# Three-product projections and logits in a gated-scan and expert kernel on one core

## The reference

```python
x  = hidden_states                      # (2, 1024, 256)
xn = layernorm(x)                       # no weights
# attention part
k  = xn @ W_z.T + b_z
log_z, log_coeffs = -softplus(-k), -softplus(k)
log_values = concat([g_log(h0), log_z + g_log(xn @ W_h.T + b_h)], axis=1)
a_star = pad(cumsum(log_coeffs, axis=-1))
log_h  = a_star + cumlogsumexp(log_values - a_star, axis=1)
log_h  = (log_h - log_h.mean()) / std(log_h)        # over everything
attn   = layernorm(exp(log_h)[:, 1:] + xn) * ln_w + ln_b
# expert part
w, e   = top_k(softmax(xn @ w_gate.T), 2); w = w / w.sum()
ffn    = sum over the 2 experts of  w * ((silu(xn @ w1.T) * (xn @ w3.T)) @ w2.T)
out    = x + attn + ffn
```

## Time and profile before

| | |
|---|---|
| median of three runs | 357.22 us |
| the profiled execution | 357.79 us, span 356.1 us |
| granted TensorE clock, mean | 0.969 |
| TensorE busy | 325.8 us, 91% of the span |
| VectorE busy | 260.8 us, 73% |
| ScalarE busy | 219.9 us, 62% |
| GpSimd busy | 206.4 us, 58% |
| chain of waits | TensorE 54%, VectorE 23%, ScalarE 8% |

### The profile page before, as it was taken

How to read it: one execution, slowest core, us unless ns; L and a number is a source line. 1 busy time by engine, 2 the same in 40 slices (tenths; PEclk the granted TensorE clock), 3 DMA queues, 4 the chain that set the end, 5 groups by cost and what they waited for, 6 DMA issues and landing times.

```text
span 356.1 us, 6682 instructions
## 1 busy us (share of the span) xinstructions
PE 325.8 (91%) x1964; PEld 273.9 (77%) x1964; DVE 260.8 (73%) x466; ACT 219.9 (62%) x328; POOL 206.4 (58%) x137
## 2 busy tenths in 40 slices
PE   8998999799999999999898999999999999979830
PEld 8883464588878898997787899889898988969730
DVE  5488787989996899889899842584589668763300
ACT  2547997455879974999854269934853485323400
POOL 4500023159968674989899728563885475945331
PEclk9999969989999999999999999999999999999985
DMA  7924912005444542354354434542463534354621
GB/s 263 426 120 137 293 52 59 15 11 150 122 82 115 142 101 32 80 129 129 44 144 109 102 38 115 142 101 33 84 181 89 75 45 76 47 76 49 98 38 15
DMA packets 19086, 37.00 MB, mean 104 GB/s; under 512 B 2272, under 2 KB 13536, under 8 KB 19008
## 3 DMA queue, kind: packets, MB, share of 16 engines
q0 software_dynamic: 9168, 11.97, 21.5%
q1 hardware_dynamic: 8496, 22.56, 20.4%
q10 hardware_dynamic: 1376, 1.85, 1.4%
HBM read 27.45 MB, written 11.03 MB: 108 GB/s over the span
## 4 chain that ended last, share of the span: by engine, by line
PE 54%; DVE 23%; ACT 8%; issue 8%; DMA 2%; ACTq 1%; POOL 1%; POOLq 0%; DVEq 0%
PE PS L1296 23%; PE PS L1314 11%; PE PS L1190 6%; PE PS L1326 5%; DVE wrow L1067 3%; DVE tmp L961 3%; PE PS L1176 2%; DMA out<-work,sidx 2%; DVE hT L956 2%; DVE U L985 2%; DVE A L998 1%; PE PS L1220 1%; DVE xrow L1054 1%; DVE xrow L1059 1%; PE PS L1265 1%
## 5 line engine op out<-in xcount | busy, mean ns | idle before, releaser
L1296 PE MATMUL PS<-wbuf,xT 128*128 128x512 f32 (+1 forms) x648 | 149.6, 384 | 4.9 <-issue 3.7
L1296 PEld LDWEIGHTS PS<-wbuf,xT 128*128 128x128 f32 x648 | 118.3, 190 | 29.4 <-issue 9.3
L424 POOL TENSOR_TENSOR wbuf<-raw,wbuf x28 | 81.4, 2924 | 23.1 <-ACT wbuf L604 21.4
L406 POOL DMA_INDIRECT out<-work,sidx x35 | 62.7, 1792 | 53.2 <-ACT work L621 20.1
L1314 PE MATMUL PS<-wbuf,hT 128*128 128x256 f32 x648 | 86.8, 288 | 0.0
L1314 PEld LDWEIGHTS PS<-wbuf,hT 128*128 128x128 f32 x648 | 79.3, 189 | 1.9 <-issue 1.9
L390 POOL DMA_INDIRECT work<-xn_dram,gidx x39 | 50.4, 1292 | 51.8 <-DVE gidx L892 36.1
L595 ACT ACTIVATE tmp<-PS 128x512 f32<-128x512 f32 x72 | 32.0, 460 | 41.6 <-PE PS L1296 41.3
L961 DVE TENSOR_TENSOR tmp<-tmp,PS 128x512 f32<-128x512 f32 x72 | 35.0, 516 | 29.4 <-ACT tmp L595 28.6
L956 DVE TENSOR_TENSOR hT<-PS,hT 128x768 fp32r<-128x768 f32 x36 | 34.2, 949 | 29.3 <-ACT hT L590 24.2
L621 ACT ACTIVATE work<-PS,wrow 128x256 f32<-128x256 f32 x35 | 16.4, 470 | 38.0 <-PE PS L1314 38.0
(11 more groups left out here) (185 smaller groups left out, 350.7 us busy)
## 6 DMA issues: line engine op xcount, KB each, us to landing
raw<-w_main SPq DMA_DIRECT2D x24, 544.0 KB
raw<-w_main SPq DMA_DIRECT2D x8, 416.0 KB
xn_dram<-xrow SPq DMA_DIRECT2D x4, 516.0 KB, 7.2
out<-xrow POOLq DMA_DIRECT2D x4, 512.0 KB, 6.1
xrow<-x SPq DMA_DIRECT2D x4, 256.0 KB, 4.8
xrow<-x ACTq DMA_DIRECT2D x4, 256.0 KB, 5.4
small_sb<-small ACTq DMA_DIRECT2D x1, 768.0 KB, 7.9
work<-xn_dram,gidx POOLq DMA_INDIRECT x39
```

The source lines that it names most:

```text
L406: pool.indirect_dma_start(out, bass.IndirectOffsetOnAxis(sidx[:, j:j + 1], 0), ysb[:, j % DEEP, :], None, compute_op=ALU.add).then_inc(s_s ...
L424: pool.tensor_tensor(lo, raw[:, ds(part, WP)], hi.bitcast(fp32), ALU.subtract).then_inc(s_w, 1)
L1296: ins = pe.matmul(PS[:, at:at + cols], xT[:, slot, xpart, q * P:(q + 1) * P], wbuf[:, w, wpart, q * 2 * F + at:q * 2 * F + at + cols], sta ...
```

## The change

Nothing of the result changes in form; three things change in how the first stage computes it.

- **Products.** The transposed input is kept as a high and a low part (`xnT_parts`, in the half of `wbuf` that the second expert fills later). ScalarE's evacuation writes the high part, VectorE subtracts it from PSUM for the low part (`xnT_low`). The projection weights and the gate weights are split too (`wzh_hi`, `wzh_lo`, `wg_parts`). A projection of 512 columns by 128 inputs becomes three "r" products (high with high, low weight with high x, high weight with low x). For the logits one product takes high x with 16 columns (both parts of the gate weights), another low x with 8; an addition joins the two sums.
- **Groups.** The first normalisation goes in eight groups of two tiles; ScalarE and GpSimd normalise one each. Fillers stand in rounds 0 to 3, the chunk-0 projections, all of them, in rounds 4 to 7.
- **Order on VectorE.** The low parts stand between the statistics and between the first expert's pieces; its third and fourth low piece go behind the tables. The one-hot tile moves from `hT` to `wbuf`.

Low parts of the input stand between the pieces, two low pieces have left this place, and the routing has one operation more. The diff, cut to its core:

```diff
-        xnT = xnT_M[:, :].rearrange("p (q n) -> p q n", q=Q)
...
+        xnT_parts = wflat[:, 2 * WALL:2 * WALL + 4 * NTOK].rearrange("p (c n q t) -> p c n q t", c=NCH, n=2, q=Q)
...
-        onehot_tile = hT[:, :, :].rearrange("p a n -> p (a n)")[:, 0:2 * NT * NCOL]
+        onehot_tile = wflat[:, 2 * WALL:2 * WALL + 2 * NT * NCOL]
+        hflat_r = hT[:, :, :].rearrange("p a n -> p (a n)")
+        wzh_hi = hflat_r[:, 0:4 * D].rearrange("p (q m d) -> p q m d", q=Q, m=2)
+        wzh_lo = [v.rearrange("p (m d) -> p m d", m=2) for v in (hflat_r[:, 4 * D:6 * D], wflat[:, 2 * WALL + 4 * NTOK:2 * WALL + 4 * NTOK + 2 * D])]
...
+        wg_parts = sb("wg_parts", [P, Q, 2, E], f32r)
...
-        logit_ps = PS[:, 7 * 512:7 * 512 + NT * E]
+        logit_ps = PS[:, 7 * 512:7 * 512 + 2 * NT * E].rearrange("p (t n e) -> p t n e", n=2, e=E)
...
+        def xnT_pair(m, part):
+
+            return xnT_parts[:, m // 2, part, :, m % 2 * 2 * P:(m % 2 + 1) * 2 * P]
...
-                pool.wait_ge(s_mr, g + 1)
-                for t in (4 * g, 4 * g + 2, 4 * g + 3):
-                    pool.tensor_scalar(xn[:, t, :], xn[:, t, :], rstd[:, t:t + 1], nmean[:, t:t + 1],
-                                       ALU.mult, ALU.add).then_inc(s_xn, 1)
+            for t in range(0, NT, 2):
+                pool.wait_ge(s_mr, t // 2 + 1)
+                pool.tensor_scalar(xn[:, t, :], xn[:, t, :], rstd[:, t:t + 1], nmean[:, t:t + 1],
+                                   ALU.mult, ALU.add).then_inc(s_xn, 1)
...
             def evacuate(m):
                 act.wait_ge(s_xtr, m + 1)
-                act.activation(xnT[:, :, 2 * P * m:2 * P * (m + 1)].rearrange("p q (t n) -> p t q n", t=2),
+                act.activation(xnT_pair(m, 0).rearrange("p q (t n) -> p t q n", t=2),
                                PS[:, (4 + m % 2) * 512:(5 + m % 2) * 512].rearrange("p (t q n) -> p t q n", t=2, q=Q),
                                ACT.Copy).then_inc(s_xnT, 1)
...
-            deviations(0)
-            normal(0)
-            deviations(1)
-            normal(1)
-            evacuate(0)
-            deviations(2)
-            normal(2)
-            evacuate(1)
-            deviations(3)
-            normal(3)
-            for m in range(2, 8):
-                evacuate(m)
+            for g in range(NT // 2):
+                deviations(g)
+                normal(g)
+                if g == 5:
+                    act.wait_ge(s_large, 16)
+                    act.activation(wzh_hi, wzh_sb, ACT.Copy).then_inc(s_wzh, 1)
+                if g >= 2:
+                    evacuate(g - 2)
+            evacuate(6)
+            evacuate(7)
...
-                group = slice(4 * g, 4 * g + 4)
+                group = slice(2 * g, 2 * g + 2)
...
-                dve.wait_ge(s_x[2 * g], 16)
-                for t in range(4 * g, 4 * g + 2):
+            def xnT_low(m):
+                dve.wait_ge(s_xnT, m + 1)
+                dve.tensor_tensor(xnT_pair(m, 1).rearrange("p q (t n) -> p t q n", t=2),
+                                  PS[:, (4 + m % 2) * 512:(5 + m % 2) * 512].rearrange("p (t q n) -> p t q n", t=2, q=Q),
+                                  xnT_pair(m, 0).bitcast(fp32)
+                                  .rearrange("p q (t n) -> p t q n", t=2), ALU.subtract).then_inc(s_xl, 1)
+
+            for g in range(NT // 2):
+                dve.wait_ge(s_x[g], 16)
+                for t in range(2 * g, 2 * g + 2):
                     ins = dve.bn_stats(bst[:, t, :], xn[:, t, :])
                 step(ins)
                 if g:
                     scales(g - 1)
-                dve.wait_ge(s_x[2 * g + 1], 16)
-                for t in range(4 * g + 2, 4 * g + 4):
-                    ins = dve.bn_stats(bst[:, t, :], xn[:, t, :])
-                step(ins)
-                for t in range(4 * g, 4 * g + 4):
+                for t in range(2 * g, 2 * g + 2):
                     ins = dve.bn_aggr(mv[:, t, :], bst[:, t, :])
                 ins.then_inc(s_var0, 1)
-            scales(3)
-            dve.wait_ge(s_small, 16)
+                if g == 3:
+                    dve.wait_ge(s_small, 16)
+                    step(dve.tensor_copy(wg_parts[:, :, 0, :], wg_sb))
+                    dve.tensor_tensor(wg_parts[:, :, 1, :], wg_sb, wg_parts[:, :, 0, :].bitcast(fp32),
+                                      ALU.subtract).then_inc(s_wg, 1)
+                if g >= 4:
+                    xnT_low(g - 4)
+                if g == 6:
+                    dve.wait_ge(s_wzh, 1)
+                    for q in range(Q):
+                        dve.tensor_tensor(wzh_lo[q], wzh_sb[:, q, :, :], wzh_hi[:, q, :, :].bitcast(fp32),
+                                          ALU.subtract).then_inc(s_wzl, 1)
+            scales(7)
+            xnT_low(4)
...
-            dve.wait_ge(s_raw, LOADS)
-            for q in range(PIECES):
+            def first_hi(q):
                 dve.tensor_copy(wbuf[:, 0, 0, q * WP:(q + 1) * WP], raw[:, q * WP:(q + 1) * WP]).then_inc(s_hi, 1)
-            for q in range(PIECES):
+
+            def first_lo(q):
                 dve.wait_ge(s_hi, q + 1)
                 hi, lo = (wbuf[:, 0, n, q * WP:(q + 1) * WP] for n in range(2))
                 dve.tensor_tensor(lo, raw[:, q * WP:(q + 1) * WP], hi.bitcast(fp32), ALU.subtract).then_inc(s_w, 1)
+            xnT_low(5)
+            dve.wait_ge(s_raw, LOADS)
+            first_hi(0)
+            first_hi(1)
+            xnT_low(6)
+            first_hi(2)
+            first_hi(3)
+            first_lo(0)
+            xnT_low(7)
+            first_lo(1)
...
-            step(dve.tensor_copy(logit, logit_ps))
+            step(dve.tensor_copy(te(logit), logit_ps[:, :, 1, :]))
+            step(dve.tensor_tensor(te(logit), te(logit), logit_ps[:, :, 0, :], ALU.add))
...
+            dve.wait_ge(s_k, 1)
...
+            first_lo(2)
+            first_lo(3)
...
-            def project(c, mat, parts=(0, 1, 2, 3)):
+            def project(c, mat, parts=(0, 1)):
 
                 base = 2 * CH * mat
                 if c and mat == 0:
                     pe.wait_ge(s_kb, 2 * c)
                 if c and mat == 1:
                     pe.wait_ge(s_yr, 4 * c)
-                for n in parts:
-                    qo, q = n // Q, n % Q
-                    ins = pe.matmul(PS[:, base + qo * CH:base + (qo + 1) * CH],
-                                    wzh_sb[:, q, mat, qo * P:(qo + 1) * P], xnT[:, q, c * CH:(c + 1) * CH],
-                                    start=(q == 0), stop=(q == Q - 1))
-                if n == 3:
+                for qo in parts:
+                    for q in range(Q):
+                        x_hi, x_lo = xnT_parts[:, c, 0, q, :], xnT_parts[:, c, 1, q, :]
+                        for wpart, rows in ((0, x_hi), (1, x_hi), (0, x_lo)):
+                            wz = (wzh_lo[q] if wpart else wzh_hi[:, q, :, :])[:, mat, qo * P:(qo + 1) * P]
+                            ins = pe.matmul(PS[:, base + qo * CH:base + (qo + 1) * CH],
+                                            wz, rows,
+                                            start=(q == 0 and rows is x_hi and wpart == 0),
+                                            stop=(q == Q - 1 and rows is x_lo))
+                if qo == 1:
...
-                pe.wait_ge(s_xnT, k + 1)
+                pe.wait_ge(s_xl, k + 1)
                 for t in (2 * k, 2 * k + 1):
                     for q in range(Q):
-                        ins = pe.matmul(logit_ps[:, t * E:(t + 1) * E], xnT[:, q, t * P:(t + 1) * P],
-                                        wg_sb[:, q, :], start=(q == 0), stop=(q == Q - 1))
+                        pe.matmul(logit_ps[:, t, :, :], xnT_parts[:, t // 4, 0, q, t % 4 * P:(t % 4 + 1) * P], wg_parts[:, q, :, :],
+                                  start=(q == 0), stop=False)
+                        ins = pe.matmul(logit_ps[:, t, 0, :], xnT_parts[:, t // 4, 1, q, t % 4 * P:(t % 4 + 1) * P],
+                                        wg_parts[:, q, 0, :], start=False, stop=(q == Q - 1))
...
-                pe.wait_ge(s_xn, 3 * (m // 2) + (3 if m % 2 else 1))
-                pe.wait_ge(s_xo, m // 2 + 1)
+                pe.wait_ge(s_xn, m + 1)
+                pe.wait_ge(s_xo, m + 1)
                 if m >= 2:
-                    pe.wait_ge(s_xnT, m - 1)
+                    pe.wait_ge(s_xl, m - 1)
                 for t in range(2):
                     for q in range(Q):
                         col = (4 + m % 2) * 512 + (t * Q + q) * P
                         ins = pe.transpose(PS[:, col:col + P], xn[:, 2 * m + t, q * P:(q + 1) * P], ident[:, :])
                 ins.then_inc(s_xtr, 1)
-                if m < 2:
+                if m < 4:
                     warm(FILL)
                 else:
-                    if m == 2:
-                        pe.wait_ge(s_large, 16)
-                        pe.wait_ge(s_xnT, 2)
-                    project(0, (m - 2) // 4, ((m - 2) % 4,))
+                    if m == 4:
```

(20 more changed lines are left out.)

5 lines of the change are left out of this document (2 added, 3 removed).

## The result

The changed kernel takes **361.72 us** (median of 4 runs, 361.31 to 362.10) against 357.22. The ratio over all their runs is 1.0116, 95% interval 1.009 to 1.0141 (the two medians alone give 1.0126). The forecast was 360.2 with a range of 357.0 to 363.0. The time lies in the range, 1.5 us above the point and 0.3 above the upper end of case A. The profiled execution took 361.57 us (span 359.8) against 357.79 (span 356.1).

The account below looks back on a forecast made before the run. It took the routing's start and VectorE's work up to the first gate as the bound. 3.25 + 0.4 - 1.45 + 2.45 - 1.64 = +3.0 gave 360.8 us against the profiled execution, 360.2 against the median; range 357.0 to 363.0.

Parts of the forecast that it names:

- case A: Whole kernel: the forecast itself holds by its own prices, time 358.8 to 361.4 us; chance 0.50.
- Term 1: First stage: waits for low parts and split weights make the last logits end at 29.3 instead of 26.05 us, +3.25 us.
- Term 2: Routing on VectorE: one more 128x128 addition with PSUM and a handover, +0.4 us.
- one chain of small steps: VectorE's routing, 26 to 40.7 us, was read as an unbroken chain of small VectorE steps.
- Term 3: One-hot loop: projections end near 43.5 us, before the loop starts at 44.3, so VectorE's wait for TensorE goes, -1.45 us.
- the loop is no longer held by TensorE: One-hot loop: second and third chunk projections are over before it starts, so its 1.45 us wait goes.
- Term 4: Between tables and first softplus: two low pieces of the first expert now stand uncovered on VectorE, +2.45 us.
- Term 5: First cumulative sum: TensorE finishes before VectorE arrives at 60.7 us, so VectorE's wait goes, -1.64 us.
- One to one from the first gate to the end: Expert loop: untouched by the change, so the first gate's shift, +3.0 us, carries to the end unchanged.
- Rival B: First stage, 11 to 29 us: TensorE's waits make its clock fall, time 361.5 to 363.2 us; chance 0.26.
- Rival C: First stage: TensorE never waits, logits end at 27.1 us, time 358.0 us, down to 357; chance 0.18.
- D: Projections: the products run no faster than float32 passes, 24 x 0.2 us ahead of the logits, 365 us; chance 0.03.

## Why the prediction was right, and where its size was off

The six steps read from the pair of profiled executions add up to the shift of the first gate: 3.12 + 0.32 - 0.59 - 0.64 + 2.41 - 1.64 = +2.98. One of them the forecast did not have.

- **Term 1, the start of the routing: +3.25 forecast, +3.12 measured.** TensorE waits for the first low part (0.82 us; the operation takes 0.66 to 0.69, forecast 0.68) and for the subtracted weights (0.61), the first projection starts at 17.36 (forecast 17.83), and the logits end at 29.2 (29.3). Errors offset each other: the warm-up ended 0.48 us earlier; a product costs 0.245 instead of 0.233 us and the first and the last logits about 0.9 instead of 0.79, but the transposes 0.41 instead of 0.49. The earlier warm-up is the execution's, not the change's: the first transposes start between 8.34 and 9.78 us in the fourteen profiled executions of both kernels and their variants. In the second execution of the change they start at 9.29, as in the kernel before; there the routing starts at 29.69, and term 1 is +3.59. The Trainium skill, "TensorE: Matmul & The Clock Gate", section "Back-to-back issue gap", has 131 ns for such a pair of load and product; the starts above don't agree. As forecast, VectorE's own list ends in the same moment, at 29.04. But VectorE waits in that list, 0.51 and 0.73 us, for copies that follow TensorE's transposes, so the two are not independent, and no run shows what a faster one of them alone would give.
- **Term 2, the addition: +0.4, measured 0.32** (29.54 to 29.86).
- **Not in the forecast: the wait for the rank matmuls, -0.59.** The prediction reads VectorE from 26 to 40.7 us as one chain of small steps; it holds a wait of 0.49 for TensorE at 31.47, which the change frees, and a handover of 0.1. This is why the one-hots start at 43.54 and not at 44.3.
- **Term 3, the one-hot loop: -1.45 forecast, -0.64 measured.** TensorE's projections were late, at half clock from 36.2 to 39.6 us. In the second execution of the change they ran at full speed from 33.8 us on and the loop started without a wait, but had two of 0.54 and 0.16 inside it, at a clock of 0.50. The step that failed is "the loop is no longer held by TensorE". Six of the profiled executions have such waits inside the loop, all with a low stretch over it.
- **Term 4, the pieces behind the tables: +2.45, measured 2.41** (52.83 to 55.24), uncovered as forecast.
- **Term 5, the wait at the cumulative sum: -1.64, and gone in the change as forecast**, at 60.65 (forecast 60.7). Against the profiled execution this is right. Against the median it is too much: the wait is 1.08 in the mean of three executions. The forecast took the profiled execution's 0.57 us above the median off its result, but kept the whole of that execution's wait as freed.
- **One to one from the first gate to the end**: +2.98 at the gate (forecast +3.0), +3.30 at the fourth tile's hidden transposes (95.80 against 92.50), +3.61 at hidden transposes near the end (332.62 against 329.01), +3.78 in the time.

Of the 0.8 us that came on top, 0.33 has a place, though no cause: the second gate comes 8.55 us behind the first instead of 8.22, because VectorE starts the low part of the first hidden tile later behind ScalarE's copy. In the kernel before:

```profile
71.83 0.81 ACT L612 ACTIVATE hT<-PS 128x768 fp32r<-128x768 f32 x1 [3.58 <-DVE plan L875]
72.74 0.96 DVE L956 TENSOR_TENSOR hT<-PS,hT 128x768 fp32r<-128x768 f32 x1 [0.95 <-ACT hT L612]
```

And with the change, 0.47 us behind the copy's end instead of 0.10:

```profile
74.80 0.81 ACT L621 ACTIVATE hT<-PS 128x768 fp32r<-128x768 f32 x1 [4.31 <-DVE plan L911]
76.08 0.96 DVE L994 TENSOR_TENSOR hT<-PS,hT 128x768 fp32r<-128x768 f32 x1 [1.30 <-ACT hT L621]
```

Seven of the eight profiled executions of the change and its variants have about 8.55 there; the six of the kernel before and its variants, and the change with the pieces on GpSimd, have 8.22 or 8.23 (groups of two alone lose as much one gate later, so it is no matter of the products). What VectorE waits for is not shown. The rest can't be told from none with one pair: the time behind the first gate lies between 288.2 and 290.9 us over the fourteen, and most of that spread stands behind the last gate (20.6 to 25.0 us).

In sum the mechanism was that of case A: every step but that of term 3 happened. That the sum at the first gate came out at +2.98 is in part luck, since the 0.81 us that term 3 gave too little and the 0.59 of the rank matmuls nearly cancel, and the change's execution had an early warm-up. Over three executions of the kernel before and two of the change the first gate is at 67.13 and 70.89 in the mean, +3.76: the start of the routing +3.30, the table +2.43 (forecast 2.2), the pieces +2.41, the freed wait -1.08. So the term that makes the forecast too low is term 5, by 0.56 us. With the 0.33 at the second gate this is +4.1, and the ratios 1.0116 and 1.0117 of the change's two sets of runs are 4.1 and 4.2 us; with so few executions the agreement may be chance.

Rival B's price fits the time, but not its place: the first stage ran at 1.00, and only the runs without fillers and with one product show B there. Rival C failed, since TensorE did wait, and D failed by the product's price.

## What to carry to other kernels

Before counting a saved TensorE pass, ask who waits for it: here all projections became cheaper at the same clock, TensorE's busy time stayed the same, and the operands' low parts went to VectorE, whose steps are the path. A wait that a change frees should be priced over several profiled executions when the engine waited for runs at a clock that falls and rises; one execution gave 1.64 us where three gave 1.08. A forecast that hits the sum is to be taken apart all the same: here a term too large by 0.81 us and a wait of 0.59 that was overlooked hid each other. Work moved "behind" something is free only if the engine has a wait there; ahead of the routing, behind the tables or on GpSimd, the two pieces of the changed kernel put 2 us or more into VectorE's chain in each place.

## What the runs showed of the hardware

Giving TensorE less to do made the kernel slower: with one product of three the granted clock fell to 0.50 at 20.3 us and stayed there 44 us, and the ratio was 1.0336 instead of 1.0116; with all three it was 1.00 until 36.2 us in one execution and 30.4 in another, so the place of the fall differs between executions of one program; without the dummy products it was 0.50 from 11.8 to 22.0. With dummy products in the gaps before the picks it fell at 45.8 in one execution, and with the same ones and more at 31.4 in another, so the fillers in the gaps do not fix the place. The Trainium skill, "TensorE: Matmul & The Clock Gate", section "A second HAM failure mode: psum-queue depth-cycling", names short idle times between groups of products as the cause of such swings; the run without fillers agrees (0.50 after idling 1.77 us), but the second execution of the change does not: its clock fell at 30.4 us though TensorE had no idle time above 0.2 us from 17.8 us on. What makes these later falls is not shown.
